# Two feed-forward layers in split float32 on one core: pair sums of the first down projection on GpSimd, and new orders around it and the norm

## What is computed

```python
gate = x @ W_gate.T + 0.5 * (x @ A_gate[idx].T) @ B_gate[idx].T      # up likewise
act = silu(gate) * up
y = act @ W_down.T + 0.5 * (act @ A_down[idx].T) @ B_down[idx].T
nx = y * rsqrt(mean(y * y) + 1e-5) * ln_w
out = x + (silu(nx @ gate_w.T) * (nx @ up_w.T)) @ down_w.T
```

## Time and profile before

| what | us |
|---|---|
| median of 3 runs (433.95 to 435.5) | 434.11 |
| the profiled execution, own time | 435.26 |
| its span, first to last instruction | 433.5 |
| TensorE busy | 398.1 |
| VectorE busy | 330.9 |
| ScalarE busy | 251.2 |
| GpSimd busy | 36.8 |

### The profile page before, as it was taken

The page is one execution under the profiler, slowest core; times in us unless marked ns, Lnnn a source line. Parts: engine busy times, 40 slices in busy tenths (PEclk is TensorE's granted clock), DMA queues, the critical chain, the costliest instruction groups (busy, mean ns, idle before and its releaser), DMA issues.

```text
span 433.5 us, 5739 instructions
## 1 busy us (share of the span) xinstructions
PE 398.1 (92%) x1954; PEld 328.1 (76%) x1954; DVE 330.9 (76%) x477; ACT 251.2 (58%) x389; POOL 36.8 (8%) x32
## 2 busy tenths in 40 slices
...
PEclk9999999998998959959977999999999999999999
...
GB/s 254 195 86 34 88 143 73 48 50 166 140 170 237 249 206 126 164 2 0 0 0 147 0 1 50 97 64 82 97 81 115 2 133 52 177 2 170 62 48 98
DMA packets 17294, 42.37 MB, mean 98 GB/s; under 512 B 2546, under 2 KB 5106, under 8 KB 17266
## 3 DMA queue, kind: packets, MB, share of 16 engines
...
q0 software_dynamic: 2784, 8.00, 10.1%
q10 hardware_dynamic: 1122, 1.84, 1.2%
...
## 4 chain that ended last, share of the span: by engine, by line
PE 65%; issue 13%; DMA 10%; DVE 6%; ACT 3%; POOL 2%; SPq 1%; POOLq 0%; DVEq 0%; ACTq 0%
PE bank L1608 41%; PE bank L1971 15%; DMA down_w_sums_raw<-wc_in 5%; PE bank L1863 3%; DVE xs L1072 2%; DMA act<-act 2%; PE bank L1618 2%; ACT stack L538 2%; DMA xa<-xT_in 1%; DMA wraw<-w_in 1%; PE bank L1802 1%; PE bank L1791 1%; POOL act L487 1%; POOL down_w_sums_raw L481 1%; DVE wx L1072 1%
## 5 line engine op out<-in xcount | busy, mean ns | idle before, releaser
L1608 PE MATMUL bank<-xs,ws 128*128 128x512 f32 x840 | 199.0, 395 | 2.9 <-ACT bank L538 1.9
L1608 PEld LDWEIGHTS bank<-xs,ws 128*128 128x128 f32 x840 | 158.9, 191 | 36.6 <-ACT bank L538 2.3
L538 ACT ACTIVATE xs<-act 128x512 fp32r<-128x512 f32 (+1 forms) x73 | 49.8, 702 | 42.0 <-DMA act<-act 14.2
L1072 DVE TENSOR_TENSOR xs<-act,xs 128x512 fp32r<-128x512 f32 (+1 forms) x66 | 53.4, 825 | 13.2 <-ACT xs L538 12.6
L1072 DVE TENSOR_TENSOR ws<-wraw,ws 128x256 fp32r<-128x256 f32 (+2 forms) x45 | 30.1, 670 | 20.1 <-ACT ws L538 20.0
L538 ACT ACTIVATE bank<-bank 128x512 f32<-128x512 f32 x34 | 19.4, 577 | 37.6 <-PE bank L1608 37.1
L1971 PE MATMUL bank<-xs,vs 128*128 128x512 f32 x168 | 38.2, 389 | 0.0
L1863 PE MATMUL bank<-xs,down_w_sums 128*128 128x512 f32 x120 | 30.5, 411 | 8.4 <-ACT bank L538 8.2
L538 ACT ACTIVATE mu<-bank 128x512 f32<-128x512 f32 x44 | 26.1, 596 | 18.2 <-PE bank L1608 12.8
L1971 PEld LDWEIGHTS bank<-xs,vs 128*128 128x128 f32 x168 | 31.5, 188 | 6.5
L1863 PE MATMUL bank<-xs,down_w 128*128 128x512 f32 x90 | 26.0, 449 | 10.1 <-issue 4.9
...
## 6 DMA issues: line engine op xcount, KB each, us to landing
wraw<-wgu_in SPq DMA_DIRECT2D x22, 512.0 KB, 3.4
down_w_sums_raw<-wc_in POOLq DMA_DIRECT2D x7, 640.0 KB, 8.5
wdr<-vs_in SPq DMA_DIRECT2D x7, 512.0 KB, 3.3
...
down_w_sums_raw<-wc_in SPq DMA_DIRECT2D x4, 640.0 KB, 4.7
act<-act POOLq DMA_DIRECT2D x4, 512.0 KB, 6.6
down_w_raw<-wc_in SPq DMA_DIRECT2D x3, 640.0 KB, 7.8
...
```

The costliest lines, as they stand in the source:

```text
L538: return nc.scalar.activation(out_ap, in_ap, ACT.Copy, scale=scale)
L1072: return nc.vector.tensor_tensor(out_ap, raw, v32(part), ALU.subtract)
L1608: ins = mm(z[:, :], w_slot(j)[:, w, s, k * P:(k + 1) * P], xs[:, c, r, k, :], start=(start and k == 0 and s == 0 and r == 0), stop=(k == 1 ...
```

## The change

**GpSimd.** The seven adding DMAs on `act` become eight tensor_tensor instructions (`pair_sum`, counted by `s_tp`), and t1's three join them; t2 is now in three parts (block 0, 1 and 2, 3). They stand in one in-order list with the seven weight DMAs; `S2_22` moves behind the two t3 sums. GpSimd also takes the three weight sums `sums(13)` (`G1 + 3`) of the norm stage, ahead of which are both its `lo_w`.

**ScalarE, VectorE.** The last `stack` parts are spread over groups 4 and 5 and `place_ad` goes from after group 4 to after group 5; C11's weights are split after group 6 (high) and in group 7 (low), t2's weights only after group 7. `sums(11)`, the halves of `w10`, `place_td`, `sums(12)`, `hi_a/b(12)`, `lo_a/b(12)`, `hi_w(C22)`, `rsqrt(0)`, the squares of the second half and `lo_b(13)` move as the diff shows; the first square of the second half goes from VectorE to ScalarE, two of the four `scale` go behind the squares.

**TensorE, SyncE.** `t_c` moves from the start of groups 6 and 7 to behind `p4(j-1)` in them. `load_w(10)` is issued ahead of the loads of C11 and t2 (both wait for `place_ad`).

```diff
             load_stack(4)
-            for j in range(7, 10):
+            for j in range(7, 11):
                 load_w(j)
             sp.wait_ge(s_ad, 10)
             load_down_w(C11, 0, 0)
             sp.wait_ge(s_stklo, 10)
             load_down_w(CT2, 0, 0)
-            load_w(10)
...
+            def pair_sum(to, more, op=ALU.add):
+                nc.gpsimd.tensor_tensor(to, to, more, op).then_inc(s_tp, 1)
+            def t2(k, end, done):
+                pool.wait_ge(s_clo, KC * C11 + end)
+                pool.wait_ge(s_tp, done)
+                pair_sum(act_c(k, end, 0), act_c(k, end, 1))
...
# ScalarE, in and after the groups
-                elif j < 4:
+                elif j < 6:
                     stack_hi(j // 2 + 2, j % 2)
-                elif j == 4:
-                    stack_hi(4, 0)
-                    stack_hi(4, 1)
-                    place_ad()
-                elif j == 5:
+                    if j == 5:
+                        place_ad()
+                elif j == 6:
                     hi_w(C11, cw_loaded(C11))
-                elif j == 6:
-                    hi_w(CT2, cw_added(S2_22))
...
             hi_w(CT3, cw_added(S3_21))
             hi_c(CT2, 0)
+            hi_w(CT2, cw_added(S2_22))
             hi_c(CT2, 1)
+            hi_c(CT2, 2)
             hi_w(C21, cw_loaded(C21))
-            hi_c(CT2, 2)
             for i in range(2):
                 seed(i)
-            for t in range(2):
-                place_td(t)
+            place_td(0)
             hi_c(CT2, 3)
             hi_c(C21, 0)
-            hi_w10(0)
-            hi_w10(1)
+            place_td(1)
             hi_c(C21, 1)
             hi_c(C21, 2)
+            hi_w10(0)
...
+            hi_w(CT1, cw_added(S1_21))
             for n in range(3):
-                hi_c(CT3, n)
-            hi_w(CT1, cw_added(S1_21))
-            hi_c(CT4, 0)
-            hi_w(C22, cw_added(S4_11))
-            hi_c(CT4, 1)
-            hi_c(CT4, 2)
+                hi_c(CT4, n)
+            nc.scalar.preload_act_table(ACT.Abs_reciprocal_sqrt)
+            hi_c(CT1, 0)
             for i in range(2):
                 copy_u3(i)
+            hi_a(G1 + 2)
...
             sum_hi(0)
+            hi_w(C22, cw_added(S4_11))
             hi_c(C22, 1)
             hi_c(C22, 2)
+            rsqrt(0)
             for i in range(2):
                 copy_p5(i)
-            rsqrt(0)
...
# VectorE
+                if j == S1 - 1:
+                    lo_w(C11)
...
                     lo_c(C11, 0)
-                    lo_w(CT2)
                     lo_c(C11, 1)
...
             c21(S1 - 1)
+            lo_w(CT2)
             lo_c(CT2, 1)
-            sums(G1 + 1)
+            lo_c(CT2, 2)
             lo_w(C21)
-            lo_c(CT2, 2)
             last_pair_sums()
             lo_c(CT2, 3)
             lo_c(C21, 0)
-            lo_w10(0)
-            lo_w10(1)
+            sums(G1 + 1)
...
             lo_t(1, 3)
+            lo_b(G1 + 3)
             c22_sum(S1)
...
# TensorE, group(j)
                     if j > 0:
                         p4(j - 1)
+                    if j == S1 - 2:
+                        pe.wait_ge(s_ad, 10)
...
+                        t_c(range(6))
+                    elif j == S1 - 1:
+                        t_c_of_pairs(3)
+                        t_c(range(6, 8))
                     p6(j)
```

More of the change, by code:

```diff
@@ L195, in build @@
         CW_ORDER = (C11, CT2, CT3, C21, CT4, CT1, C22)
+        CW_HI = (C11, CT3, CT2, C21, CT4, CT1, C22)
         def cw_loaded(p):
@@ L688, in hi_c @@
                 if name == "t2":
-                    for half in range(k // 2, (end - 1) // 2 + 1):
-                        a.wait_ge(*((s_last, 2) if half == 2 else t_added(T2_01 + half)))
+                    a.wait_ge(*((s_tp, T2_0 + n) if n < 3 else (s_last, 2)))
                 elif name == "t3":
-                    a.wait_ge(*t_added(T3_012 + k // 3))
+                    a.wait_ge(s_tp, (T3_012, T3_012, T3_3)[n])
                     if end == KC:
@@ L1004, in _ @@
             sum_hi(0)
+            hi_w(C22, cw_added(S4_11))
             hi_c(C22, 1)
             hi_c(C22, 2)
+            rsqrt(0)
             for i in range(2):
                 copy_p5(i)
-            rsqrt(0)
             a.wait_ge(s_nx, 2)
             hi_x(1, X11, nx0[:, 0:2, :])
+            square(4)
+            square(5)
+            hi_a(G1 + 3)
+            square(6)
+            sum_hi(1)
             a.wait_ge(s_nx, 4)
             hi_x(1, X21, nx0[:, 2:4, :])
-            for j in range(G1 + 2, G1 + 4):
-                hi_a(j)
-                hi_b(j)
-            for m in range(5, 7):
-                square(m)
-            sum_hi(1)
             square_hi()
+            hi_b(G1 + 3)
             ca(S1)
@@ L1478, in _ @@
             lo_a(G1 + 1)
+            lo_c(CT3, 0)
+            lo_c(CT3, 1)
+            lo_w10(1)
+            lo_c(CT3, 2)
             lo_b(G1 + 1)
-            for n in range(3):
-                lo_c(CT3, n)
+            sums(G1 + 2)
             for n in range(3):
@@ L1484, in _ @@
             lo_c(CT1, 0)
+            v.wait_ge(s_lnw, 16)
+            nc.vector.tensor_scalar(lnw[:, :], lnw[:, :], 0.375 / (H * H), 0.0, ALU.mult, ALU.add).then_inc(s_lnws, 1)
+            lo_a(G1 + 2)
             add_square(0, 1)
             lo_c(CT1, 1)
+            lo_b(G1 + 2)
             add_square(0, 2)
```

178 lines of the change are left out of this document (81 added, 97 removed).

## The result

| | before | after |
|---|---|---|
| median, us (runs) | 434.03 (4) | 419.75 (4) |
| lowest to highest | 432.41 to 435.5 | 418.88 to 420.65 |
| span of the profiled run | 433.5 | 418.5 |
| TensorE / VectorE / GpSimd busy | 398.1 / 330.9 / 36.8 | 394.2 / 348.4 / 52.6 |

The ratio is 0.967, with a 95% interval of 0.963 to 0.972. Forecast were 417.1 us and a gain of 17.0; the two medians differ by 14.3 us and the two spans by 15.0.

A forecast was written before the change was run, and what follows sets the result against it. TensorE was taken to set the time, its idle gaps and the slow clock behind them being winnable. Eight terms summed to a 17.0 us gain, from a median of 434.1 to 417.1 us; range 406 to 426, the forecast's own 411 to 423.

The forecast's parts named there:

- 4, t2's product at full clock: At t2's product: without the gap ahead its matmuls take 7.1 us instead of 9.02, gaining 1.8 us.
- One and two: Groups up to product 11: place_ad's gap and slow clock go (3.6 us), and product 11's operands come earlier (1.9 us).
- Three: From product 11 to t2's product: GpSimd sums replace t2's DMA, a 2.0 us wait for VectorE remains; gain 6.3 us.
- Five: From product 21 to t1's product: VectorE's and GpSimd's work adds up, t1's product starts at 185.2; gain 0.5 us.
- six: From t1's product to product 22's end: later weights and GpSimd's sums(13) cost 4.0 us.
- serial end: Before t1's product: VectorE's and GpSimd's lists in series, 36 us, give the low half of t1's weights at 185.2.
- GpSimd's list goes first: Bound for t1's product: 193.7 if GpSimd goes first each time, TensorE waiting 9 us; running gain 5.6 us.
- Seven and eight: Norm after product 22: VectorE work leaves the stretch to q2(8), gain 7.6 us; then lo_b(13) ahead of c22_sum(8) costs 0.7.
- Little collides: Rival, chance 0.18: VectorE and GpSimd fit into each other's pauses, TensorE alone sets the stage; 405.7 us.
- The change does nothing it says: Rival, chance 0.05: waits of 8.24 and 4.93 us stay because weight DMAs land as late as the sums did; 425.7 us.
- GpSimd always goes first: Rival, chance 0.20: VectorE waits for GpSimd each time around t2's and t1's products; gain 8.5 us, 425.6 us.
- Slower: Rival, chance 0.04: GpSimd's sums stretch and its list becomes the bound; 442 us at twice their length.

The follow-up runs named there:

- e4_dma: The changed kernel with the sums of t3, t2 and t4 made by adding DMAs again, all new orders kept: 422.71 us, ratio 0.976.
- e5_groups: The kernel before the change with only the part around the groups (place_ad, t_c, weight halves and load_w(10) moved): 439.87 us, ratio 1.016.
- e7_groups: The kernel before the change with the part around the groups alone, plus GpSimd's weight DMAs in the changed kernel's order: 435.80 us, ratio 1.007.
- e12_all_vector: The changed kernel with t1's and t4's sums, t2's second and third and lo_w(CT1) on VectorE, t3's and t4's operands split earlier: 407.03 us, ratio 0.940.
- e10_t1_vector: The changed kernel with t1's three pair sums and lo_w(CT1) on VectorE instead of GpSimd: 411.95 us, ratio 0.951.
- e1_hold: The changed kernel with GpSimd holding t1's last sum and lo_w(CT1) until VectorE has made t3's low parts: 417.86 us, ratio 0.965.
- e2_hold_all: The changed kernel with t4's last sum and all t1's sums on GpSimd held behind VectorE's splits of t3's operands: 418.33 us, ratio 0.967.
- e8_early: The changed kernel with t3's operands split earlier on ScalarE and VectorE, right behind product 21's operands: 418.21 us, ratio 0.965.
- e3_wait2: The changed kernel with a second, long satisfied wait ahead of GpSimd's lo_w(CT1): 419.21 us, ratio 0.967.

## Why the prediction was right, and where it was off

| term | predicted, us | measured, us |
|---|---|---|
| 1 and 2, product 11 starts | 5.5 | 136.72 - 131.25 = 5.47 |
| 3, t2's product starts | 6.3 | 156.68 - 145.84 - 5.47 = 5.4 |
| 4, t2's product at full clock | 1.8 | 1.9 |
| 5, t1's product starts | 0.5 | 199.32 - 190.99 - 12.7 = -4.4 |
| 6, product 22 ends | -4.0 | 8.3 - 8.3 = 0.0 |
| 7, `q2(8)` | 7.6 | 16.3 - 8.3 = 8.0 |
| 8, the rest | -0.7 | 15.0 - 16.3 = -1.3 |
| sum | 17.0 | 15.0 |

**One and two** came to the tenth in their sum: `place_ad` is off the path (TensorE runs through 97 us at full clock) and product 11 starts at 131.25 for 131.2. Missed was that t3's first sum on GpSimd (3.82 us) would stretch `lo_b(9)` and give a wait of 0.63 us at 118.64; e4_dma, e5_groups and e7_groups, without that sum, have no such wait and start product 11 0.8 to 1.5 us earlier. So the orders alone win up to 7.0 us here and GpSimd takes some of it back; that 5.5 came out to the tenth is luck. Left out too was that these two terms count only together with the third.

**Three.** The wait of `p4(7)` was 2.16 us for the 2.0 taken; VectorE's instruction at 131.78 was issued 0.1 us behind the start of the second sum (131.65), waited for it and got in ahead of the third. The clock behind that gap was not priced. The assumption that instructions with a PSUM operand are free held (0.68 us at 131.06 and 134.50). e12_all_vector took this term further: from product 11 to t2's product 11.7 us, for 14.6.

**Five, the step that failed, and six with it.** The serial end was nearly right: 185.2 had been taken for both lists together, and VectorE's was through at about 181.8. What failed was its use as the start of t1's product. Serial lists set when the last of them is done, but TensorE waits for each operand in turn. GpSimd was through t4's and t1's sums and `lo_w(CT1)`, which I had placed last, by 171.44; VectorE's share came behind it. So t3's first operand, not t1's weights, was late, and from t3's start TensorE needed its own 18.9 us. The bound "GpSimd's list goes first" had t3's first part at 170.8 and 9 us of wait; it was 172.14 and 12.37. As a result term six's cost did not come. The prediction had product 22 start 12.0 us behind t1's (no working is shown for the 12.0), so at 197.2; its weights were there at 198.05 (195.09 + 2.96), 7.1 us behind t1's late start, and it started at 199.75 without a wait:
```profile
195.09 2.96 POOL L485 TENSOR_TENSOR down_w_sums<-down_w_sums_raw,down_w_sums 128x1280 fp32r<-128x1280 f32 x1 [23.65 <-ACT down_w_sums L546]
```
In e12_all_vector, where t1's product starts early, the distance is 11.3 us, as term six had it. So term five promised 4.9 us too much and term six took off 4.0 that did not come; five and six were 3.5 us of loss together and 4.4 was measured. That the total lies 2.0 us from the forecast, and not 6, rests on these two errors meeting, which the prediction had not reckoned with.

**Seven and eight.** 8.0 for 7.6 and -1.3 for -0.7. In the eighth, a slow clock behind the norm (15 matmuls 4.68 us, for 3.92 before) comes on top of the 0.55 us wait at 238.51.

**The rivals.** "Little collides" fell: each split of 1024 columns would keep 1.22 us and t3 would start at 160. "The change does nothing it says" fell: the waits of 8.24 and 4.93 us are gone. "GpSimd always goes first" had the right mechanism at t3 (and t1's product, at 190.99, lies nearer to its 193.7 than to the forecast's 185.2) and too high a price for what follows. "Slower" fell: GpSimd's eleven sums average 2.4 us, for the 2.3 that the earlier trace rows made them; it is VectorE that waits. The mechanism that the forecast and "GpSimd always goes first" share, two lists run one after the other, is the one the runs bear out: doing four instructions of the shared list on the faster engine, 4.5 us for some 10, gave 8.3 us (e10_t1_vector), while moving the list about (e1_hold, e2_hold_all, e8_early) gave 0 to 2 in the medians.

The Trainium skill (SBUF — State Buffer, section "SBUF: two separate sides") describes a VectorE instruction with two SBUF inputs and a GpSimd instruction as shutting each other out of a shared port pair for a whole instruction; the row at 131.78 agrees, 2.80 us for 0.69. It names the holder by who starts first. With both waiting, the traces show two cases: one VectorE instruction gets in between two GpSimd ones (3.39 us in e8_early), or none does (5.85 us at 166.15, though issued 2.2 us ahead of the second GpSimd instruction). e3_wait2 excludes the number of waits as the reason. What decides it stays open.
